# A Perceiver kernel on one core: seven more value units projected early, and a one-head cross attention whose scores lie with keys on partitions

## The chip, the cores and the metric

The kernel runs on one core of one Trainium2 chip. The metric is the device time of one execution in microseconds (us), median of three executions. Engines are called by the names of the profile: PE is TensorE (PEld its weight loads), DVE is VectorE, ACT is ScalarE, POOL is GpSimd, and SP is SyncE, whose queue issues every DMA of this kernel.

## What is computed

Twelve layers update `x` (128 tokens x 256). Each is `x = x + layer(layernorm(x), ...)`: four groups (L0 to L3) of a cross attention ("x"), a self attention ("a") and a feed-forward layer ("f"). The cross attentions read a context `ctx_1024` of 12544 rows x 256, the same for all. The change touches three of them:

```python
# L0x: a linear layer on x and on the mean of the context
# L1x: ONE head, the keys and the values are the context rows themselves
#   score[q, key] = sum_d (x[q,d]*w3[d] + w2[d]) * ctx[key,d]  +  row[q]
#   attended[q]   = softmax over the 12544 keys of score, times ctx
#   bat           = softmax over the queries of each query's largest score;  hc = bat-weighted mean of x
#   out           = [x, attended, x*attended, x*hc] @ W_qv + b
# L2x: 16 heads of 16
def _L2_xattn_ref(Q, K, V, mask, Wq, bq, Wk, bk, Wv, bv, Wo, bo):
    q = _split_heads(Q @ Wq.T + bq)
    k = _split_heads(K @ Wk.T + bk)
    v = _split_heads(V @ Wv.T + bv)          # V is the context: the "value units" below are pieces of this
    scores = jnp.einsum('bhqd,bhkd->bhqk', q, k) * scale
    scores = jnp.where(mask == 0, -jnp.inf, scores)
    attn = jax.nn.softmax(scores, axis=-1)
    return jnp.einsum('bhqk,bhkd->bhqd', attn, v)...  @ Wo.T + bo
```

All of it is in fp32.

## The kernel before, in words

The context is cut into 7 chunks of 1792 keys (`NC`, `CH`), each in two halves of 896 (`HC`). A **value unit** (c, b) is 256 keys of chunk c times `Wv` of L2x: 4 matmul instructions of 128x256 (each shows as two MATMUL records in the trace, since fp32 takes two passes), 7 units a chunk, 49 in all. A unit depends only on the context and `Wv`, so it can be made long before L2x. Every engine runs its own instruction list in the order in which the code writes it; semaphores join them.

- **L0x** (0 to 41 us) streams the 7 chunks for the mean. While a chunk is in SBUF, PE projects units b = 0 and 1 of chunks 0, 2, 3, 4, 5 and 6 (`PASSING`, L1095). **L0a** (41 to 72 us) fills PE's waits with the 5 units of `AFTER` (`after`, L730, taken by ACT at L1428). `KEPT["L2x"]` says how many units of each chunk are made ahead; they lie in `arena` and `mask_bias`, and SP writes them to DRAM (`held_out`) with two DMAs (L508, L509), which stand in SP's queue ahead of the first experts of L0f. Where there is no such work PE runs `warm` (L702), products of the identity that nobody reads.
- **L0f** (75.8 to 139 us): 8 experts of 1408 KB up and 768 KB down weights, 3 buffers in `wide`; L696 is the up product, L1034 the down product.
- **L1x** (139 to 256 us). First pass: 14 halves; for each, the query matrix `x2T` is the stationary operand and the keys are streamed (L1200: 512 and 384 columns, two halves of the depth), so a score tile is 128 queries x 896 keys. DVE (L2064) adds `row`, writes the tile to `arena` and takes its largest value. Then the largest score of each query is known along the free axis (L2068, L2069). Second pass: ACT exponentiates a tile with the accumulated sum (L1497), PE turns its 7 blocks (`turn`, L691), DVE and ACT copy them from PSUM to `pT` (L2081, L1507), and PE multiplies the turned blocks by the context rows (`multiply`, L1229). SP loads the halves (L451, L517) and the rows (L535, four buffers in `wide`). Between the passes PE has `warm(T2[:, 1], 20)`.
- **L1a, L1f** (256 to 314 us): chunk 1's seven units of L2x are made here (`early`, L714).
- **L2x** (314 to 843 us): `cross`. A prologue projects the keys and the values of chunk 0 (`key_unit` L826, `value_unit` L839), then 56 pairs of heads (7 chunks x 8 pairs) each do scores (L854), softmax, 7 groups of 4 turns (L868), and the product with the values (`multiply`, L891). The plan (`Plan.values_of`) puts the missing value units of chunk c+1 into pairs 0, 2, 3, 4 and 6 of chunk c. Kept units come back from DRAM (`load_held`, L564). **L3x** has the same form and keeps none.

Of the kernel before, what the change touches and what calls it, by code (L numbers as in the profile page):

```python
# [17 lines left out]
ALU = mybir.AluOpType  # L18
ACT = mybir.ActivationFunctionType
# [61 lines left out]
def stage_lists(layers):  # L81
# [7 lines left out]
    for layer in layers:  # L89
# [21 lines left out]
        elif layer == "L1x":  # L111
            add(layer, dve=["A", "AT", "max", "gmax", "bat", "f", "fT"], pe=["AT_ps", "hc_ps", "fT_ps", "out"],
                pool=["gmax"], act=["bat"])
# [29 lines left out]
WHOLE = 4  # L143
KEPT = {"L2x": [0 if c == 1 else 7 if c == WHOLE else 2 for c in range(7)], "L3x": [0] * 7}
# [53 lines left out]
DUMPED = 4  # L198
# [4 lines left out]
assert KD * D + (len(HELD) - IN_ARENA) * 2 * D <= CH  # L203
# [4 lines left out]
def build(nc, a, layers=LAYERS):  # L208
    ctx = ExitStack()
    with ctx:  # L210
# [179 lines left out]
        for layer in layers:  # L390
            if layer == "L0x":
                sems(layer, "first_in0", "first_in1", "first_in2", "second_in0", "second_in1", "second_in2",
                     "first_summed", "second_summed", "wv_in", "held_ready", "held_taken", "held_out",
                     "after_ready", "after_taken")
            elif layer == "L1x":
                sems(layer, "ctx_in0", "ctx_in1", "ctx_in2", "ctx_in3", "s_ready", "s_taken", "p_ready", "nat_in0", "nat_in1", "nat_in2", "nat_in3", "t_ready", "t_dve", "t_act",
# [16 lines left out]
        held_b = mask_bias[:, KD * D:KD * D + (len(HELD) - IN_ARENA) * 2 * D].rearrange("p (u n) -> p u n", n=2 * D)  # L413

        def held(of):

            n = HELD.index(of)
            return held_a[:, n] if n < IN_ARENA else held_b[:, n - IN_ARENA]
# [8 lines left out]
        def _(sp):  # L427
# [51 lines left out]

            def load_early(of):  # L480
# [8 lines left out]
            for i, layer in enumerate(layers):  # L489
                prev = layers[i - 1] if i else None  # L490
                if layer == "L0x":
# [14 lines left out]
                    sp.wait_ge(s["held_taken"], len(PASSING))  # L506
                    sp.wait_ge(s["after_taken"], len(AFTER))
                    sp.dma_start(held_out[:, 0:IN_ARENA], held_a).then_inc(s["held_out"], 16)  # L508
                    sp.dma_start(held_out[:, IN_ARENA:len(HELD)], held_b).then_inc(s["held_out"], 16)  # L509
                elif layer == "L1x":  # L510
# [13 lines left out]
                    if i + 1 < len(layers):  # L524
                        load_pack(layers[i + 1])
                    with sp.Fori(1, NC // 2) as n:
# [10 lines left out]
                    for n in range(2 * NC):  # L537
                        if n >= 4:
                            sp.wait_ge(s["pv_ready"], n - 3)
                        load_nat(n)  # L540
                    sp.wait_ge(s["s_ready"], 2 * NC)
                    load_early("L2x")
                elif layer in ("L2x", "L3x"):
# [14 lines left out]
                    def load_held(c):  # L558

                        n, units = HELD.index((c, 0)), plan.kept[c]  # L560
                        sp.wait_ge(L["L0x"]["held_out"], 32)
# [73 lines left out]
                elif layer in FF:  # L635
# [5 lines left out]
                    for e in range(n, E):  # L641
# [3 lines left out]
                        load_down(layer, e)  # L645
                if i + 1 < len(layers) and layers[i + 1] != "L3f" and (layers[i + 1] in FF or layers[i + 1] == "L1f"):

                    if prev:
                        need(sp, "dve", f"{prev}.end")
# [1549 lines left out]
```

## Time and profile before

| what | value |
|---|---|
| median of three executions | 1581.24 us (1580.27 to 1581.38) |
| the profiled execution, its own time | 1574.64 us |
| its span in the profile | 1573.0 us |
| PE / PEld busy | 1498.3 us (95%) / 1125.8 us (72%) |
| DVE / ACT busy | 957.5 us (61%) / 941.3 us (60%) |
| shares of the chain that ended last | PE 81%, DVE 7%, issue 5%, ACT 5%, DMA 2% |
| HBM read / written | 161.33 MB / 4.59 MB |

The chain that ended last is followed back from the last instruction to what released each one; a share of 81% for PE says that for that part of the span the end waited for matmuls. Times inside the text are microseconds from the start of the span.

### The profile page before, as it was taken

To read this page: it belongs to the slowest core of one execution; us is meant where nothing else is said; L and a number is where in the kernel's file an instruction comes from. 1 tells how busy PE (TensorE), PEld (TensorE's weight loads), DVE (VectorE), ACT (ScalarE), POOL (GpSimd) and SP (SyncE) were. 2 spreads that over 40 slices of the span, in tenths; PEclk is the share of its full clock that TensorE was granted. 3 is DMA by queue.
4 is the path that set the end of the run, shared out by engine and by line. 5 is a ranking of instruction groups with operands and counts; after the bars stand their busy time and mean duration, and the time that the engine had idled before them with its cause. 6 is when DMAs were issued, how large, how long until landed. Compare 5 with 4: busy or idle time off the path is not lost.

```text
span 1573.0 us, 34356 instructions
## 1 busy us (share of the span) xinstructions
PE 1498.3 (95%) x14142; PEld 1125.8 (72%) x14142; DVE 957.5 (61%) x1828; ACT 941.3 (60%) x1439; POOL 9.7 (1%) x22
## 2 busy tenths in 40 slices
PE   6999998999999999999998999999999999998899
PEld 5797587767777766777776876777777777776664
DVE  5523323658767787777775216776767676767632
ACT  3110041248887888787883215877777777778711
POOL 0000000000000000000000000000000000000000
PEclk9999999899999999999999999999999999999999
DMA  9595764274534353444314547443434343423346
GB/s 394 230 371 217 277 219 193 84 264 152 183 133 171 129 189 126 147 160 144 114 47 168 210 176 253 146 162 117 143 119 141 118 142 118 142 95 124 128 178 265
DMA packets 56169, 270.88 MB, mean 172 GB/s; under 512 B 6608, under 2 KB 6864, under 8 KB 49360
## 3 DMA queue, kind: packets, MB, share of 16 engines
q1 hardware_dynamic: 56016, 268.70, 46.5%
q8 instruction: 113, 1.85, 0.5%
q14 instruction: 40, 0.33, 0.1%
HBM read 161.33 MB, written 4.59 MB: 105 GB/s over the span
## 4 chain that ended last, share of the span: by engine, by line
PE 81%; DVE 7%; issue 5%; ACT 5%; DMA 2%; POOL 0%; SPq 0%; DVEq 0%; ACTq 0%
PE T L868 14%; PE O L891 9%; PE S L854 8%; PE O L868 7%; PE T L826 7%; PE T L839 5%; PE S L696 5%; PE O L826 3%; PE S L1200 3%; PE O L1229 3%; PE O L696 2%; PE T L691 2%; PE O L839 2%; ACT sc L1315 2%; DVE sc L1742 2%
## 5 line engine op out<-in xcount | busy, mean ns | idle before, releaser
L1742 DVE CUSTOM_DVE_ANT_0 sc<-S,mask_bias,small 128x896 f32<-128x896 f32 x336 | 377.5, 1149 | 46.9 <-PE S L854 46.9
L1315 ACT ACTIVATE sc<-sc,small 128x1792 f32<-128x1792 f32 x168 | 300.1, 1786 | 2.5 <-DVE small L1742 1.0
L1301 ACT ACTIVATE pT<-T 128x512 f32<-128x512 f32 x366 | 212.3, 597 | 87.3 <-PE T L868 87.3
L868 PE MATMUL T<-consts,sc 128*128 128x128 f32 x1546 | 232.7, 281 | 5.0 <-ACT sc L1315 3.1
L891 PEld LDWEIGHTS O<-pT,arena 128*32 128x32 f32 x6272 | 164.8, 110 | 74.8 <-issue 72.3
L868 PEld LDWEIGHTS T<-consts,sc 128*128 128x128 f32 x1546 | 168.9, 141 | 61.0 <-issue 39.8
L891 PE MATMUL O<-pT,arena 128*32 128x128 f32 x6272 | 194.4, 274 | 9.0 <-ACT pT L1301 9.0
L854 PE MATMUL S<-keys,q 64*128 64x512 f32 (+1 forms) x896 | 151.2, 414 | 10.1 <-DVE small L1742 9.9
L1708 DVE COPY pT<-T 128x512 f32<-128x512 f32 x150 | 103.5, 690 | 79.4 <-PE T L868 78.6
L1301 ACT ACTIVATE pT<-O 128x512 f32<-128x512 f32 x194 | 115.9, 597 | 52.4 <-PE O L868 52.4
L826 PE MATMUL T<-ctx_in,packs 128*128 128x448 f32 x320 | 135.1, 547 | 1.1 <-issue 1.1
L868 PE MATMUL O<-consts,sc 128*128 128x128 f32 x806 | 129.3, 281 | 1.6 <-ACT pT L1301 1.4
L1742 DVE CUSTOM_DVE_ANT_0 packs<-S,mask_bias,small 128x896 f32<-128x896 f32 x112 | 128.1, 1144 | 0.0
L868 PEld LDWEIGHTS O<-consts,sc 128*128 128x128 f32 x806 | 89.2, 141 | 33.4 <-issue 24.3
L854 PEld LDWEIGHTS S<-keys,q 64*128 64x128 f32 x896 | 67.2, 185 | 50.3 <-issue 40.4
L1315 ACT ACTIVATE packs<-packs,small 128x1792 f32<-128x1792 f32 x56 | 99.6, 1779 | 0.0
L839 PE MATMUL T<-packs,ctx_in 128*128 128x256 f32 x384 | 90.3, 379 | 0.0
L826 PEld LDWEIGHTS T<-ctx_in,packs 128*128 128x128 f32 x320 | 55.7, 192 | 35.5 <-issue 35.5
L868 PE MATMUL T<-consts,packs 128*128 128x128 f32 x518 | 78.8, 280 | 1.7 <-ACT pT L1301 1.7
L839 PEld LDWEIGHTS T<-packs,ctx_in 128*128 128x128 f32 x384 | 69.7, 190 | 7.7
L1708 DVE COPY pT<-O 128x512 f32<-128x512 f32 x74 | 51.0, 690 | 35.5 <-PE O L868 34.8
L696 PEld LDWEIGHTS S<-xT,wide 128*128 128x128 f32 x608 | 69.5, 192 | 2.3 <-issue 2.0
(369 smaller groups left out, 1803.1 us busy)
## 6 DMA issues: line engine op xcount, KB each, us to landing
keys<-keys_hl SPq DMA_DIRECT2D x224, 448.0 KB, 4.4
ctx_in<-in_ctx_cols SPq DMA_DIRECT2D x46, 896.0 KB, 4.7
wide<-in_ctx_rows SPq DMA_DIRECT2D x14, 896.0 KB, 4.6
wide<-in_up_L0f SPq DMA_DIRECT2D x8, 1408.0 KB, 13.0
sc<-in_ctx_cols SPq DMA_DIRECT2D x10, 896.0 KB, 5.5
wide<-in_up_L2f SPq DMA_DIRECT2D x8, 1024.0 KB, 7.1
wide<-in_down_L2f SPq DMA_DIRECT2D x8, 1024.0 KB, 5.0
wide<-in_up_L3f SPq DMA_DIRECT2D x4, 2048.0 KB, 8.1
```

The lines of the kernel that those rows point to most:

```text
L696: last = mm(out, lhsT[:, k, :], rhs[:, k, :], start=(k == 0), stop=(k == n - 1))
L826: last = mm(ring(plan, u)[:, 0:HC // 2], wk[:, k, hf * P:(hf + 1) * P], ctx_in[:, nb // 2, k, (nb % 2) * (HC // 2):(nb % 2 + 1) * (HC // 2 ...
L839: last = mm(ring(plan, u)[:, (t % 2) * D:(t % 2 + 1) * D], ctx_in[:, half, k, at * P:(at + 1) * P], wv[:, k, :], start=(k == 0), stop=(k = ...
L854: last = mm(S4f[:, i * 2 * BANK + n0:i * 2 * BANK + n1], q4[own, j, :], keys4[own, j, half * HC + n0:half * HC + n1], start=True, stop=True)
L868: last = nc.tensor.transpose(ring(plan, u)[:, t * P:(t + 1) * P], weights_of(2 * m + i)[:, b * P:(b + 1) * P], ident)
L891: last = mm(O2[32 * g:32 * g + 32, 1, at:at + P], vv[:, c % 2, b, j * 32:(j + 1) * 32], pT2[:, t * P:(t + 1) * P], start=(b < 4), stop=(b ...
L1200: last = mm(S4f[:, q % 2 * 2 * BANK + n0:q % 2 * 2 * BANK + n1], x2T[:, k, :], half_in(q)[:, k, n0:n1], start=(k == 0), stop=(k == KD - 1))
L1229: last = mm(O2[:, 0, 0:D], pT[:, 2 * (n % 2) + t // 4, t % 4 * P:(t % 4 + 1) * P], wide[:, (n % 4) * HC * KD + t * D:(n % 4) * HC * KD + ( ...
L1301: nc.scalar.activation(pT2[:, g * BANK:(g + 1) * BANK], ring(plan, u), ACT.Copy).then_inc(s["t_act"], 1)
L1315: nc.scalar.activation(weights_of(n), weights_of(n), ACT.Exp, bias=n_best[c % 2][:, h:h + 1], scale=-1.0, accum_out=l_new[c % 2][:, h:h + ...
L1708: V.tensor_copy(pT2[:, g * BANK:(g + 1) * BANK], ring(plan, u)).then_inc(s["t_dve"], 1)
L1742: V.tensor_tensor_reduce(weights_of(n)[:, i * HC:(i + 1) * HC], S4f[:, n % 2 * 2 * BANK:n % 2 * 2 * BANK + HC], mask_bias[:, i * HC:(i + 1 ...
```

## The change

Kept value units of L2x go from 17 to 24 (`KEPT["L2x"]` from `[2, 0, 2, 2, 7, 2, 2]` to `[4, 0, 2, 2, 7, 2, 7]`): units 2 and 3 of chunk 0, and 2 to 6 of chunk 6. Three of them, (6,2) to (6,4), join `AFTER` in L0a; four are `LATE` and are made in L1x, from halves of the context that L1x has in SBUF. The prologue of L2x then has 3 value units in place of 5, and chunk 5 none in place of 5. The dumps are one DMA of 256 KB for each unit (2 KB a partition) in place of two large ones: 17 ahead of L0f's experts, 3 at L0f's end, 4 in L1x.

L1x is rewritten: each block of 128 keys is now the stationary operand and the queries are streamed, so a score tile has keys on partitions. ACT moves it to `arena`, DVE keeps an elementwise maximum (`folded`); after the last half the fold goes over the 7 blocks, through a PE transpose and a reduction, and the broadcast maximum is turned into `T2[:, 1]`. The second pass subtracts it (`lower`, DVE), exponentiates in place (ACT), adds up the sums elementwise (`add_up`, DVE) and multiplies at once: no turns and no copies of turned blocks. The sum over keys is 7 one-column products at the end (`total_ps`). ACT now loads the table of Exp inside L1x.

```diff
-KEPT = {"L2x": [0 if c == 1 else 7 if c == WHOLE else 2 for c in range(7)], "L3x": [0] * 7}
+KEPT = {"L2x": [4, 0, 2, 2, 7, 2, 7], "L3x": [0] * 7}
+LATE = [(0, 2), (0, 3), (6, 5), (6, 6)]
...
-AFTER = [(c, b) for c, b in HELD if b >= 2]
+AFTER = [(c, b) for c, b in HELD if b >= 2 and (c, b) not in LATE]
+FIRST_OUT = PASSING + AFTER[0:5]
...
+            def dump(units, done):
+                for u in units:
+                    sp.dma_start(held_out[:, HELD.index(u)], held(u)).then_inc(L["L0x"][done], 16)
...
                     load_pack(layers[1])
-                    sp.wait_ge(s["held_taken"], len(PASSING))
-                    sp.wait_ge(s["after_taken"], len(AFTER))
-                    sp.dma_start(held_out[:, 0:IN_ARENA], held_a).then_inc(s["held_out"], 16)
-                    sp.dma_start(held_out[:, IN_ARENA:len(HELD)], held_b).then_inc(s["held_out"], 16)
...
+                    if layers[i + 1] == "L0f":
+                        sp.wait_ge(L["L0x"]["held_taken"], len(PASSING))
+                        sp.wait_ge(L["L0x"]["after_taken"], 5)
+                        dump(FIRST_OUT, "held_out")
...
+                elif layer == "L1x":
+                    late(0, S4[:, 2])
+                    warm(T2[:, 0], 7)
                 elif layer != layers[0]:
                     warm(T2[:, 0], 11)
...
                     after(1, S4[:, 3])
-                    warm(T2[:, 1], 5)
+                    after(2, S4[:, 1])
...
+                elif layer == "L0a":
+                    after(7, S4[:, 1])
                 else:
                     warm(S4[:, 0], wait)
...
-                        pe.wait_ge(L["L0x"]["after_taken"], len(AFTER))
-                        warm(O2[:, 1], 11)
+                        after(6, T2[:, 1], 4)
+                        warm(O2[:, 0], 8)
+                        pe.wait_ge(L["L0x"]["after_taken"], 6)
...
-                        for n0, n1 in ((0, BANK), (BANK, HC)):
-                            for k in range(KD):
-                                last = mm(S4f[:, q % 2 * 2 * BANK + n0:q % 2 * 2 * BANK + n1], x2T[:, k, :],
-                                          half_in(q)[:, k, n0:n1], start=(k == 0), stop=(k == KD - 1))
+                        for t in range(TH):
+                            last = product(S4f[:, n % 2 * 2 * BANK + t * P:n % 2 * 2 * BANK + (t + 1) * P],
+                                           half_in(q)[:, :, t * P:(t + 1) * P], x2T)
...
-                    warm(T2[:, 1], 20)
-                    turn(0)
-                    for n in range(1, 2 * NC):
-                        turn(n)
-                        multiply(n - 1)
+                    late(2, O2[:, 0])
+                    need(pe, "dve", f"{layer}.fold")
+                    done("pe", transposes(T2[:, 0], work[:, 0:P], 1), f"{layer}.fold_ps")
+                    need(pe, "dve", f"{layer}.m")
+                    done("pe", transposes(T2[:, 1], work[:, 256:256 + P], 1), f"{layer}.m_ps")
...
+                    late(3, O2[:, 1])
+                    pe.wait_ge(L["L0x"]["late_taken"], 3)
+                    for n in range(2 * NC):
+                        multiply(n)
...
+                    need(pe, "dve", f"{layer}.total")
+                    for t in range(TH):
+                        last = mm(S4[:, 2, 0:1], sc[:, 2, t * P:(t + 1) * P], work[:, 512 + D:512 + D + 1],
+                                  start=(t == 0), stop=(t == TH - 1))
+                    done("pe", last, f"{layer}.total_ps")
...
...
+                    def lower(n):
+                        at = n * HC
+                        dve.wait_ge(s["moved"], n + 1)
+                        for n0, n1 in ((0, 4 * P), (4 * P, HC)) if n == 0 else ((0, HC),):
+                            piece = arena[:, at + n0:at + n1].rearrange("p (t n) -> p t n", n=P)
+                            V.tensor_tensor(piece, piece, bcast(T2[:, 1, 0:P], (n1 - n0) // P, False), ALU.subtract) \
+                                .then_inc(s["lowered"], 1)
+                    def add_up(n):
+                        dve.wait_ge(s["p_ready"], n + 2)
+                        other = arena[:, 0:HC] if n == 1 else folded
+                        ins = V.tensor_tensor(folded, other, arena[:, n * HC:(n + 1) * HC], ALU.add)
```

How the change moves instructions, as the two programs have them. **PE, from the end of L0f to the second pass of L1x.** `T`, `O` and `S` are PSUM; line numbers are those of each file. Before (the same four rows of L1200 go on through a loop), from the last product of L0f's experts:

```order
L1034 MATMUL O<-wide,arena 128x256 x12
L702 MATMUL T<-consts 128x128 x11
L691 MATMUL T<-consts,xn 128x128 x2
L702 MATMUL O<-consts 128x128 x9
L691 MATMUL T<-consts,x 128x128 x2
L1200 MATMUL S<-ctx_in,x2T 128x512 x2
L1200 MATMUL S<-ctx_in,x2T 128x384 x2
...
L702 MATMUL T<-consts 128x128 x20
L691 MATMUL T<-consts,sc 128x128 x14
L1229 MATMUL O<-wide,pT 128x256 x7
L691 MATMUL T<-consts,sc 128x128 x7
```

And in the changed kernel (L774 is `late`, L730 `warm`, L719 transposes, L1276 `multiply`):

```order
L1085 MATMUL O<-wide,arena 128x256 x12
L774 MATMUL S<-mask_bias,ctx_in 128x256 x4
L730 MATMUL T<-consts 128x128 x7
L719 MATMUL T<-consts,xn 128x128 x2
L774 MATMUL S<-mask_bias,ctx_in 128x256 x4
L719 MATMUL T<-consts,x 128x128 x2
L724 MATMUL S<-x2T,ctx_in 128x128 x28
...
L774 MATMUL O<-mask_bias,ctx_in 128x256 x4
L719 MATMUL T<-consts,work 128x128 x2
L774 MATMUL O<-mask_bias,ctx_in 128x256 x4
L1276 MATMUL O<-wide,arena 128x256 x21
```

The 7 turns before every group of 7 products are gone, a half of the first pass is 14 products of 128 columns in place of 4 of 512 or 384, and the 20 products of `warm` between the passes are replaced by two late units and two single transposes.

**SP, between L0a's weights and L0f's experts**, with the semaphores that each waits for. Before:

```order
L435 DMA packs<-in_pack_L0a 128x4352
L508 DMA held_values<-arena 128x7680 [waits L0x_after_taken,L0x_held_taken]
L509 DMA held_values<-mask_bias 128x1024
L435 DMA packs<-in_pack_L0f 128x16 [waits dve_stages]
L456 DMA wide<-in_up_L0f 128x2816 [waits dve_stages]
```

And now:

```order
L448 DMA packs<-in_pack_L0a 128x4352
L448 DMA packs<-in_pack_L0f 128x16 [waits dve_stages]
L496 DMA held_values<-arena 128x512 [waits L0x_after_taken,L0x_held_taken]
L496 DMA held_values<-arena 128x512 x9
L496 DMA held_values<-mask_bias 128x512 x2
L496 DMA held_values<-arena 128x512 x5
L469 DMA wide<-in_up_L0f 128x2816 [waits dve_stages]
```

Two DMAs ahead of the first expert's weights have become seventeen, with the same bytes.

**ACT, in L1x.** Now (L1552 takes a late unit, L1562 moves a score tile, L1572 is Exp):

```order
L1552 ACTIVATE mask_bias<-S 128x512 x2
L1562 ACTIVATE arena<-S 128x896 x14
L1552 ACTIVATE wide<-O 128x512
L1572 ACT_TABLE_LOAD
L1572 ACTIVATE arena<-arena 128x512
L1572 ACTIVATE arena<-arena 128x384
L1552 ACTIVATE wide<-O 128x512
L1572 ACTIVATE arena<-arena 128x896
```

Before, the table load stood right behind the last expert's activations of L0f; now it stands between the 14 moves and the first Exp.

## Rows read from the trace of the kernel before

**Rows 1.** The page, its busy line and the chain that ended last.

```profile
PE 1498.3 (95%) x14142; PEld 1125.8 (72%) x14142; DVE 957.5 (61%) x1828; ACT 941.3 (60%) x1439; POOL 9.7 (1%) x22
...
PE 81%; DVE 7%; issue 5%; ACT 5%; DMA 2%; POOL 0%; SPq 0%; DVEq 0%; ACTq 0%
```

**Rows 2.** The chain in order of time: start us, us, engine, output, line, records.

```profile
64.71 3.49 PE O L1127 x32
...
96.60 5.11 PE S L696 x44
...
145.91 42.36 PE S L1200 x112
196.09 3.02 PE O L1229 x14
199.88 3.02 PE O L1229 x14
```

**Rows 3.** Timeline, L1x: start, us, engine, line, operation, records [idle before <-releaser].

```profile
142.11 0.44 PE L691 MATMUL T<-consts,xn 128*128 128x128 f32 x2 [0.40 <-DVE xn L1535]
...
188.11 4.63 PE L702 MATMUL T<-consts 128*128 128x128 f32 x40
...
195.92 3.19 PE L1229 MATMUL O<-wide,pT 128*128 128x256 f32 x14
...
248.14 0.48 DVE L2098 TENSOR_SCALAR arena<-O,small 128x256 f32<-128x256 f32 x1 [5.48 <-PE O L1229]
```

**Rows 4.** Stretches: us, busy (x records) of PE, PEld, DVE, ACT, POOL, PEclk, DMA share, GB/s.

```profile
322.00:324.00 2.00, 2.00 (x8) 1.19 (x7) 0.75 (x2) 0.92 (x2) 0.00 (x0) 1.00 0.36 140
...
559.86:626.81 66.95, 65.77 (x785) 47.28 (x785) 54.51 (x103) 57.20 (x86) 0.00 (x0) 1.00 0.51 180
...
702.08:777.35 75.27, 74.09 (x826) 54.76 (x825) 54.96 (x103) 60.62 (x91) 0.00 (x0) 1.00 0.38 130
...
292.00:296.00 4.00, 2.90 (x9) 2.12 (x9) 3.04 (x4) 0.00 (x0) 0.00 (x0) 0.50 0.00 0
```

**Rows 5.** Timeline, the prologue of L2x.

```profile
327.12 1.89 PE L839 MATMUL T<-packs,ctx_in 128*128 128x256 f32 x8
...
335.85 0.67 PE L854 MATMUL S<-keys,q 64*128 64x512 f32 x4
```

**Rows 6.** Timeline, L0a and the start of L0f.

```profile
58.26 2.72 PE L702 MATMUL O<-consts 128*128 128x128 f32 x22
...
61.01 3.70 PE L806 MATMUL S<-pT,arena 128*128 128x512 f32 x8
...
75.79 10.13 PE L696 MATMUL S<-xT,wide 128*128 128x128 f32 x88
```

**Rows 7.** DMA issues: size of one, us from issue to landing (the experts' from 60:60.5).

```profile
held_values<-arena SPq DMA_DIRECT2D x1, 3840.0 KB, 12.2
...
mask_bias<-in_pack_L3x SPq DMA_DIRECT2D x1, 256.0 KB, 2.5
...
wide<-in_up_L0f SPq DMA_DIRECT2D x1, 1408.0 KB, 15.3
```

**Rows 8.** DMA queue in 176:190 and 324.5:333: packets, MB, share of 16 engines.

```profile
q1 hardware_dynamic: 796, 5.03, 89.1%
...
q1 hardware_dynamic: 951, 3.01, 102.7%
```

**Rows 9.** Timeline, prices of DVE and ACT forms in L0a and L1a.

```profile
54.67 0.69 DVE L1902 TENSOR_TENSOR work<-work,x 128x512 f32<-128x512 f32 x1
...
57.61 0.60 ACT L1428 ACTIVATE arena<-S 128x512 f32<-128x512 f32 x1 [1.13 <-PE S L730]
58.61 2.35 DVE L1585 TENSOR_TENSOR pT<-T,consts 128x1024 f32<-128x1024 f32 x2
...
268.45 1.28 ACT L1450 ACT_TABLE_LOAD   x1
...
269.75 0.23 ACT L1450 ACTIVATE small<-small 128x32 f32<-128x32 f32 x1
```

More of the change, by code:

```diff
@@ L732, in after, with late @@
                 last.then_inc(s["after_ready"], 1)
+            def late(n, bank):
+                s = L["L0x"]
+                c, b = LATE[n]
+                halves = L["L1x"]
+                if c == 0:
+                    pe.wait_ge(halves["ctx_in0"], 16)
+                    if 2 * b + 1 >= TB // 2:
+                        pe.wait_ge(halves["ctx_in1"], 16)
+                for t in (2 * b, 2 * b + 1):
+                    part, at = divmod(t, TB // 2)
+                    for k in range(KD):
+                        last = mm(bank[:, (t % 2) * D:(t % 2 + 1) * D], ctx_in[:, part, k, at * P:(at + 1) * P],
+                                  early_wv[:, k, :], start=(k == 0), stop=(k == KD - 1))
+                last.then_inc(s["late_ready"], 1)
             def norm(layer):
@@ L1123, in _ @@
                         pe.wait_ge(L["L3x"]["early_taken"], 4)
+                    else:
+                        pe.wait_ge(L["L0x"]["after_taken"], 7)
                     for b in range(4):
@@ L1186, in _ @@
                     s = L[layer]
-                    warm(O2[:, 1], 9)
+                    late(1, S4[:, 3])
                     need(pe, "dve", f"{layer}.A")
@@ L1411, in take_early, with take_after @@
                                      ACT.Copy).then_inc(s["early_taken"], 1)
+            def take_after(n, bank):
+                act.wait_ge(L["L0x"]["after_ready"], n + 1)
+                nc.scalar.activation(held(AFTER[n]), bank, ACT.Copy).then_inc(L["L0x"]["after_taken"], 1)
             for layer in layers:
@@ L2067, in _ @@
-                    dve.wait_ge(s["s_taken"], 2 * NC)
-                    link(V.tensor_reduce(row_max, maxes, X, ALU.max))
-                    done("dve", V.tensor_scalar(rec, row_max, -1.0, None, ALU.mult), f"{layer}.max")
+                    folded = sc[:, 2, 0:HC]
+                    fold, fold_last = work[:, 0:P], work[:, P:2 * P]
+                    for n in range(2 * NC):
+                        last = n == 2 * NC - 1
+                        dve.wait_ge(s["s_ready" if last else "moved"], n + 1)
+                        src = S4f[:, n % 2 * 2 * BANK:n % 2 * 2 * BANK + HC] if last else arena[:, n * HC:(n + 1) * HC]
+                        if n:
+                            dve.wait_ge(s["s_taken"], n)
+                        if n == 0:
+                            V.tensor_copy(folded, src).then_inc(s["s_taken"], 1)
+                        elif not last:
+                            V.tensor_tensor(folded, src, folded, ALU.max).then_inc(s["s_taken"], 1)
+                            if n == 2 * NC - 2:
+                                dve.wait_ge(s["s_taken"], n + 1)
+                                link(V.tensor_reduce(fold, folded.rearrange("p (t n) -> p n t", n=P), X, ALU.max))
+                        else:
+                            V.tensor_reduce(fold_last, src.rearrange("p (t n) -> p n t", n=P), X, ALU.max) \
+                                .then_inc(s["s_taken"], 1)
@@ L2090, in _ @@
+                    for n in range(1, 2 * NC):
+                        if n + 2 < 2 * NC:
+                            lower(n + 2)
+                        add_up(n)
+                        if n == 4:
                             need(dve, "pe", f"{layer}.hc_ps")
```

186 lines of the change are left out of this document (107 added, 79 removed).

## The prediction

> **What bounds the kernel now.** I read the page first: PE is busy for 95% of the span and carries 81% of the chain that ended last [rows 1], so a change pays where it takes matmuls off PE, or a wait of PE's. Then the chain in order of time, for L1x: the first pass is one run of PE, 112 records of L1200 in 42.2 us from 145.91 to 188.11, 3.01 us a half, and the second repeats with a period of 3.79 us, of which the products with the context are 3.02 and the turns and their handover the rest [rows 2, 3]. Then the stretches of L2x: chunk 5 with five value units takes 75.27 us, chunk 3, which has none, 66.95, both with PE busy for over 98% [rows 4]. Last the timelines around L0f's start, between the passes of L1x, and in L2x's prologue.
>
> This is summed against the profiled execution, 1574.64 us. The three runs have the median 1581.24, 6.6 us above it; I take the difference over unchanged.
>
> **L0a and the norm of L1x: +1.1.** A value unit on PE is 1.75 us (five in 8.73 us from 327.12 to 335.85 [rows 5]); a record of `warm` is 0.12 (22 in 2.72 [rows 6]).
> - Second norm of L0a: a unit in place of 10 warm records, 0.5 longer, mostly inside DVE's normalisation. I take 0.1.
> - Ahead of the head products: a unit (from 58.1) and 16 warm records (1.9) in place of 22. PE is free at 61.75, where it began L806 at 61.01 [rows 6]: +0.7. L0a's tail: the unit ends as DVE's result comes, 0.
> - First norm of L1x: 1.75 + 14 x 0.12 from 139.0 is 142.4, the transposes began at 142.11 [rows 3]: +0.3. `late(1)` (1.75) is shorter than the 18 records that it replaces, 0.
>
> **The dumps ahead of L0f: 0.** They now go in 17 DMAs with rows of 2 KB. The first expert's weights landed 15.3 us after their issue at 60.1, that is at 75.4, and PE began with them at 75.79 [rows 6, 7]: only 0.4 of slack, so this counts. Against it, the dumps wait for five units of `AFTER`, and one unit was moved earlier, so they start 1.7 sooner; and L0a ends 0.8 later. Price of the small rows: a packet took 250 ns in the stretch whose packets average 6.3 KB (796 packets, 89.1% of 16 engines x 14 us) and 147 ns where they average 3.2 KB (951, 102.7% of 16 x 8.5 us) [rows 8], 33 ns for each KB, so one of 2 KB is an estimated 110 ns; 17 x 128 of them on 16 engines make 15.0 us. Before, the dumps took about 13.2 (from 58.8 to the landing of the weights less 3.4 for their own bytes). 1.8 us more against 0.4 + 1.7 + 0.8 of slack: hidden. Bounds: 0, and +4 if small packets cost twice what I put on them over the large ones.
>
> **First pass of L1x: +3.3.** Weights of 128x128 with 128 moving columns are exactly L0f's up product: 44 records in 5.11 us, 0.116 each [rows 2]. A half is 14 calls, 28 records, 3.25 us, against 3.01: 14 x 3.25 = 45.5 against 42.2. ACT's move of 896 columns (about 0.9, from 0.60 for 512 [rows 9]) and DVE's maximum (about 1.1, from 0.69 for 512 [rows 9]) hide beside it. The late dumps are 0.5 MB beside PE's pass; cover enough.
>
> **Between the passes: -3.0.** Before, 188.11 to 195.92, 7.8 us [rows 3]. Now, from the last half's end: DVE's reduction of it to +1.2 and the last maximum to +1.45, `late(2)` on PE to +1.95, a transpose to +2.2, reduction and broadcast copy to +2.75, transpose to +3.2, `lower` of 512 columns to +3.9 (0.69 [rows 9]), Exp to +4.6, product at about +4.8. The table load (1.28 [rows 9]) runs from +2.7, behind `late(2)`'s copy, and is done at +4.0, just in time. A load from 268.45 is followed by the next activation at 269.75, 0.02 us behind its end [rows 9]. The Trainium skill, page "ScalarE: Activation LUTs", section "What ACT_TABLE_LOAD costs", adds a drain of 1380 ns to each switch; by that Exp would start at +5.4 and the sum would be 1.4 us smaller. The row does not bear it out, so the sum goes by 1.28.
>
> **Second pass: -9.3.** 14 groups at 3.02 plus 0.5 for the batch product: 42.8, against 52.1 (195.92 to 248.03). This holds if DVE keeps up: `lower` with PSUM as one operand about 1.05 (1024 columns take 1.17 [rows 9]), `add_up` 1.1, 2.2 us a half against 3.02. Exp, on ACT, costs about what the move does. The context rows arrive at 0.9 MB every 3.02 us, 304 GB/s, under the 403 GB/s which the stretch 176:190 reaches at full share (5.03 MB in 14 x 0.89 us [rows 8]).
>
> **Tail of L1x: +1.8.** DVE began the division at 248.14, 0.1 behind the last product. Now 14 one-column records stand between, at the 0.11 of L1127's 17-column records (32 in 3.49 [rows 2]), 1.6, and a reciprocal of 0.2.
>
> **Prologue of L2x: -3.5.** Two units of 1.75. The scores then want the first half's keys at 332.3. The queue was at 0.36 share in 322:324 [rows 4], so the 0.5 MB more of kept values (1.2 us) fits into that gap and the key copies start when they did. Bounds: -3.5 and 0.
>
> **Chunk 5: -8.3.** 75.27 - 66.95 [rows 4]. The load of seven units for chunk 6 is what chunk 4 does now. Certain but for a few tenths.
>
> Sum: 1.1 + 0 + 3.3 - 3.0 - 9.3 + 1.8 - 3.5 - 8.3 = **-17.9 us**. Profiled execution 1556.7, median **1563.3 us**, -1.1%. A change under 0.2%, about 3 us, could not be told from none.
>
> **Rivals.**
> - *L0f starts late.* The dumps run slower than estimated and every microsecond beyond 1.1 spare goes on the path. For: the spare is small, and the second expert has no more. Against: the earlier start. At +4: 1567.3. Chance 0.15.
> - *DVE bounds the second pass.* If the broadcast operand of `lower` makes both operations cost 1.7 us, the period is 3.5, +0.5 x 12 = +6: 1569.3. No row shows more than 1.2 for such a form. 0.06.
> - *L2x's prologue waits for its keys,* so the two units come out of a wait: +3.5, 1566.8. For: DMA share is about 1.0 from 324 to 333. Against: before, nothing waited there, PE came from its value units straight to the scores [rows 5]. 0.10.
> - *PE's clock falls elsewhere.* It was granted 0.50 (1.2 GHz) in 292:296, where PE was busy 2.90 of 4 us [rows 4]; the same work two stages later may meet it for more or less of the time, and L1x's tail now has matmuls of one column. 2 us either way, in the range; no case of its own.
> - *The small dumps do not overlap (slower).* If each 256 KB dump is finished before the next moves, it costs at least the 2.5 us of such a DMA [rows 7]: 17 x 2.5 = 42.5 us in place of 13.2, less 2.9 of slack, L0f starts 26.4 us late: and the median is 1589.7. It decides against the change from 34 us for the dumps, 2.0 each. Against: the key copies, 448 KB each, have four in flight and reach a share of 1.0 [rows 8]. The Trainium skill, page "DMA: Bandwidth & Descriptors", section "Bandwidth", says to batch DMAs to 1 MiB or more for 75% of peak, which speaks against this edit; its fit in "Anatomy of one DMA" makes 256 KB an estimated 2.6 us, 44 us for 17 in a row, with 17 x 2.6 - 16.1 the sum would end at +10 and the median at 1591. No row here shows DMAs of one queue kept apart. 0.03.
> - *The gain is there but the shift sets off other waits* (1567 to 1573), 0.06.
>
> **How the numbers follow.** Forecast 0.60; the cases above 0.15, 0.06, 0.10, 0.03, 0.06. The likeliest gives 1563.3. Eight in ten: downward the clock and a faster handover between the passes, 4 us; upward the late L0f and the prologue together, 7.5 us: 1559.3 to 1570.8. Faster by more than 0.2%: 0.95; within: 0.02; slower: 0.03.
>
> **What would show it.** In the profile after: first pass 45 to 46 us, PE solid; the first product 4.5 to 5.5 us behind its end; groups of 14 products 3.02 apart with no idle PE; division 1.8 us behind the last; L0f's first product within 1 us of where L0a's end puts it, else the dumps are the cause; five units' worth, 8.3 us, missing in chunk 5; the first scores of L2x right behind three value units. Wrong if the second pass's period is over 3.2 us, if ACT waits behind its table load, or if PE idles ahead of L0f's first product.

## The result, and the profile after

| what | before | after |
|---|---|---|
| median | 1580.76 us (4 executions: 1575.37, 1580.27, 1581.24, 1581.38) | 1556.03 us (4: 1554.82, 1555.73, 1556.34, 1559.02) |
| the profiled execution, its span | 1574.64, 1573.0 us | 1554.82, 1553.0 us |
| mean granted clock of the profiled execution | 0.992 | 0.992 |

The ratio is 0.9854, with a 95% interval of 0.9828 to 0.988: 1.5% faster. I had said 1563.3 us (1559.3 to 1570.8), so the sign was right and the gain was larger than even the low end. Against the profiled execution, on which the sum was made, I had said 1556.7 and 1554.82 came.

The page of the changed kernel, its busy line and chain (against [rows 1]):

```profile
PE 1480.4 (95%) x14248; PEld 1129.8 (73%) x14248; DVE 976.6 (63%) x1830; ACT 945.6 (61%) x1426; POOL 9.7 (1%) x22
...
PE 80%; DVE 8%; issue 5%; ACT 5%; DMA 2%; POOL 0%; SPq 0%; DVEq 0%; ACTq 0%
```

PE is still the bound, with 17.9 us less busy time, and DVE has 19.1 us more. The chain of L1x in order of time (start us, us, what), against [rows 2, 3]:

```profile
146.00 40.93 PE S L724 x364
186.92 0.02 issue
186.95 0.93 ACT arena L1562
187.87 0.02 issue
187.90 1.10 DVE sc L2140
189.00 0.02 issue
189.02 1.71 DVE work L2143
190.74 0.02 issue
190.76 1.10 DVE work L2145
...
193.37 1.28 ACT L1572
194.65 0.01 issue
194.66 0.64 ACT arena L1572
```

The chain leaves PE a half early, at 186.9: from there DVE decides when the second pass can begin, and last the table load. The timeline of the turnaround, the second pass and the tail (start, us, engine, line, operation, records [idle before <-releaser]):

```profile
189.87 1.89 PE L774 MATMUL O<-mask_bias,ctx_in 128*128 128x256 f32 x8
190.76 1.09 DVE L2145 TENSOR_REDUCE work<-S 128x128 f32<-128x896 f32 x1
195.44 9.30 PE L1276 MATMUL O<-wide,arena 128*128 128x256 f32 x42 [0.17 <-ACT arena L1572]
...
205.01 33.40 PE L1276 MATMUL O<-wide,arena 128*128 128x256 f32 x154
...
238.25 1.62 PE L1292 MATMUL S<-work,sc 128*128 128x1 f32 x14
239.90 0.17 DVE L2195 RECIPROCAL small<-S 128x1 f32<-128x1 f32 x1 [15.77 <-PE S L1292]
240.11 0.48 DVE L2197 TENSOR_SCALAR sc<-O,small 128x256 f32<-128x256 f32 x1
```

The late unit of L774 stands directly behind the last scores, so the first pass ends at 189.87. DVE has the last scores there too, but begins to reduce them at 190.76. The second pass is two runs of L1276, 196 records (14 halves of 14), with only the two records of the batch product between them, and 14 records take 3.02 us as forecast. In the tail the reciprocal's 15.77 us of idle time say that DVE's own part of the sum was ready long before.

The prologue of L2x (against [rows 5]) and chunk 5 of L2x (691.94 to 758.90, with chunk 3 above it; against [rows 4]):

```profile
320.38 1.89 PE L890 MATMUL T<-packs,ctx_in 128*128 128x256 f32 x8
322.11 1.89 PE L890 MATMUL O<-packs,ctx_in 128*128 128x256 f32 x8
323.84 1.89 PE L890 MATMUL T<-packs,ctx_in 128*128 128x256 f32 x8
325.66 0.67 PE L905 MATMUL S<-keys,q 64*128 64x512 f32 x4
```

```profile
549.72:616.67 66.95, 65.77 (x786) 47.31 (x785) 54.53 (x103) 57.21 (x86) 0.00 (x0) 1.00 0.50 180
691.94:758.90 66.96, 65.77 (x786) 47.30 (x785) 54.53 (x103) 57.22 (x86) 0.00 (x0) 1.00 0.47 166
```

Three units and then the scores, without a gap; and chunk 5 is now chunk 3 to 0.01 us.

**Where the time went**, by the same place in both traces:

| step | before | after | said | measured |
|---|---|---|---|---|
| start of the first pass | 145.91 | 146.00 | +1.1 | +0.1 (the stream of L0x ended 0.6 sooner this time; +0.7 without that) |
| first pass | 42.2 | 43.87 | +3.3 | +1.7 |
| between the passes | 7.81 | 5.57 | -3.0 | -2.2 |
| second pass | 52.1 | 42.8 | -9.3 | -9.3 |
| last product to division | 0.1 | 1.86 | +1.8 | +1.8 |
| L1a and L1f (half clock there longer) | | | none | +1.3 |
| prologue of L2x | | | -3.5 | -3.5 |
| chunk 5 of L2x | 75.27 | 66.96 | -8.3 | -8.3 |
| behind chunk 5 (before had a half clock at 844) | | | none | -1.5 |
| sum | 1573.0 | 1553.0 | -17.9 | -20.0 |

The last row but one is this stretch of before (us, busy (x records) of PE, PEld, DVE, ACT, POOL, PEclk, DMA share, GB/s), which has no like in the profile after:

```profile
844.00:846.00 2.00, 2.00 (x6) 1.58 (x5) 1.19 (x4) 0.00 (x0) 0.39 (x1) 0.51 0.06 10
846.00:848.00 2.00, 2.00 (x10) 1.71 (x9) 0.41 (x1) 0.46 (x1) 0.16 (x1) 0.64 0.87 267
```

The clock is at its lower level (1.2 GHz of 2.4) for most of this, which takes 2 x 0.49 + 2 x 0.36 = 1.7 us from PE. So step by step the mechanism is the one forecast, and the sum is off by 2.1 us in all; single terms are off by up to 1.6, and the half clock added 1.3 in L1a and L1f and saved 1.5 behind chunk 5. What is left is that the medians lie 24.7 us apart and the two profiled executions 19.8, and the experiments began there.

### The profile page after: what moved, and what is told of

It is laid out like the page before. It is cut to its first block, busy times and chain, and to the rows that moved or that the text cites. A ratio compares the mean times of both kernels' runs of the same rounds, so it can differ in the third digit from the quotient of the medians.

```text
span 1553.0 us, 34523 instructions
## 1 busy us (share of the span) xinstructions
PE 1480.4 (95%) x14248; PEld 1129.8 (73%) x14248; DVE 976.6 (63%) x1830; ACT 945.6 (61%) x1426; POOL 9.7 (1%) x22
## 4 chain that ended last, share of the span: by engine, by line
PE 80%; DVE 8%; issue 5%; ACT 5%; DMA 2%; POOL 0%; SPq 0%; DVEq 0%; ACTq 0%
PE T L919 14%; PE O L942 9%; PE S L724 8%; PE S L905 8%; PE O L919 7%; PE T L877 7%; PE T L890 5%; PE O L1276 3%; PE O L877 3%; PE O L724 2%; PE O L890 2%; ACT sc L1366 2%; PE S L1014 2%; DVE sc L1811 2%; PE T L719 2%
## 5 line engine op out<-in xcount | busy, mean ns | idle before, releaser
L1352 ACT ACTIVATE pT<-T 128x512 f32<-128x512 f32 x360 | 208.9, 598 | 82.6 <-PE T L919 82.6
L1777 DVE COPY pT<-T 128x512 f32<-128x512 f32 x155 | 106.9, 690 | 85.8 <-PE T L919 85.2
L905 PE MATMUL S<-keys,q 64*128 64x512 f32 (+1 forms) x896 | 150.9, 414 | 10.2 <-DVE small L1811 10.0
L1352 ACT ACTIVATE pT<-O 128x512 f32<-128x512 f32 x200 | 119.5, 597 | 55.2 <-PE O L919 55.2
L877 PE MATMUL T<-ctx_in,packs 128*128 128x448 f32 x332 | 140.2, 547 | 1.1 <-issue 1.1
L890 PE MATMUL T<-packs,ctx_in 128*128 128x256 f32 x328 | 77.2, 379 | 0.0
L724 PE MATMUL S<-xT,wide 128*128 128x128 f32 x608 | 70.9, 276 | 0.0
L919 PEld LDWEIGHTS T<-consts,packs 128*128 128x128 f32 x516 | 56.4, 141 | 15.1 <-issue 9.8
```

Source lines behind the costliest of these rows:

```text
L724: last = mm(out, lhsT[:, k, :], rhs[:, k, :], start=(k == 0), stop=(k == n - 1))
L877: last = mm(ring(plan, u)[:, 0:HC // 2], wk[:, k, hf * P:(hf + 1) * P], ctx_in[:, nb // 2, k, (nb % 2) * (HC // 2):(nb % 2 + 1) * (HC // 2 ...
L890: last = mm(ring(plan, u)[:, (t % 2) * D:(t % 2 + 1) * D], ctx_in[:, half, k, at * P:(at + 1) * P], wv[:, k, :], start=(k == 0), stop=(k = ...
L905: last = mm(S4f[:, i * 2 * BANK + n0:i * 2 * BANK + n1], q4[own, j, :], keys4[own, j, half * HC + n0:half * HC + n1], start=True, stop=True)
L919: last = nc.tensor.transpose(ring(plan, u)[:, t * P:(t + 1) * P], weights_of(2 * m + i)[:, b * P:(b + 1) * P], ident)
L1352: nc.scalar.activation(pT2[:, g * BANK:(g + 1) * BANK], ring(plan, u), ACT.Copy).then_inc(s["t_act"], 1)
```

## Experiments

**How times are compared here.** Executions of one kernel scatter widely (those of before from 1574.3 to 1588.5 us). Each comes with its span and mean granted clock, and their product is the time that it would have taken at the full clock, called the full-clock time below. It is an estimate (the clock has three digits, and not every microsecond is PE's), but its mean is steadier than a median. The +- behind it is the standard error of that mean.

**1. Both kernels again, unchanged.**

> The kernel before, unchanged, to see its own scatter. Theory A: its executions lie on two levels, 1574.5 to 1576 and 1580 to 1582 us, as the five times known so far do (1574.64, 1575.37, 1580.27, 1581.24, 1581.38), and the upper level has a lower mean granted clock (about 0.988 against 0.992), so the 6.6 us between its profiled execution and its median is TensorE time at the half clock, and no property that a change keeps. Theory B: the timed executions all lie at 1580 to 1582 and only the profiled one is shorter; then the offset belongs to the way of timing, and the changed kernel's own 1.2 us would need another reason.

> The changed kernel, unchanged. Theory A: 1554.5 to 1559.5 us, median near 1556, with the longer ones at a lower mean clock (0.989 against 0.992). Theory B: all timed executions within 1 us of each other.

Measured: the kernel before 1574.3 to 1583.15 us, median 1578.4 of 12. The executions at 0.992 took 1574.3 to 1575.3 and those at 0.986 and 0.987 took 1581.3 to 1583.2, with all values between: not two levels, but a time that goes with the clock. The changed kernel took 1556.95 and 1557.15 (0.992), 1560.46 (0.989) and 1561.35 (0.988). Theory A stands in what matters and B falls; but two of these four lie above the 1559.5 that I had given as their upper end, and their median, 1558.8, above the 1556. With the runs of before that came beside all later experiments there are 74 executions of it (median 1578.8, full-clock 1560.1 +-0.1) and 8 of the changed kernel (median 1557.1, full-clock 1541.6 +-0.4): the change is worth **18.6 us at equal clock**, where the sum said 17.9. At 0.992 alone the means are 1575.1 (10) and 1556.2 (5), 18.9 apart.

**2. L1x alone, and the seven units made but not used.** The first is the kernel before with the new L1x, without `late`. The second is the changed kernel with one line:

```diff
-        self.kept = KEPT[layer]
+        self.kept = [2, 0, 2, 2, 7, 2, 2] if layer == "L2x" else KEPT[layer]
```

> The kernel before with the rewritten L1x only: 17 kept value units, the two large dumps and the prologue and chunk 5 of L2x as before; warm products stand where the late units stood. By the two traces L1x is worth 8.1 us (its last products -8.03 against before, of which L0a and the start +0.1): profiled execution 1566.5 us, L2x 1.3 us earlier or later by the clock. My forecast's terms (first pass +3.3, between -3.0, second -9.3, tail +1.8) would make it 1567.4. If the units made in L1x cost it time, for example through DMA or ACT, this comes out lower, under 1565.

> The changed kernel, which makes and dumps all 24 units, but L2x's plan takes only the old 17 from DRAM and projects the other seven again in its prologue and in chunk 5. By the trace these seven are worth 3.5 + 8.3 = 11.8 us: profiled execution 1566.6 us, within 1 us of the run with L1x alone, since making the units early costs only the 0.6 us by which the head products of L0a start later. Rival: the units take part of their gain back where they are made (L0a, L1x, the dumps); then this run is longer than the one with L1x alone by over 1.5 us.

Measured: medians 1570.2 us and 1571.5 us, both 0.9949 of before (0.9935 to 0.9964), full-clock 1551.9 +-0.4 and 1553.0 +-0.3. L1x alone gains 8.2 (said 8.1). Using the seven units gains 11.4 (1553.0 to 1541.6; said 11.8), making them costs 1.1 +-0.5 (said 0.6; the rival's 1.5 is not excluded by this). The parts add up by construction, since each run is compared with the one before it; what is tested is the size of each. Both profiled executions had the clock at 0.989, which is why their own times, 1569.8 and 1571.5, are 3 and 5 us above what I wrote.

**3. The tail of L1x.**

```diff
+ # DVE, behind the last add_up
+ V.tensor_reduce(fold, folded.rearrange("p (t n) -> p n t", n=P), X, ALU.add)
  # PE, ahead of the last multiply; the seven products behind it are gone
+ mm(S4[:, 2, 0:1], work[:, 0:P], work[:, 512 + D:512 + D + 1], start=True, stop=True)
```

> The changed kernel with the sum over keys folded on DVE first (one reduction over the 7 blocks, DVE being idle for 15.8 us there), so that one one-column product, put ahead of the last half's products, takes the place of seven behind them. If the tail's +1.8 us is the 14 records and the reciprocal behind the last product, the division begins 0.1 us behind that product in place of 1.86, and L1x's tail (last product to the output product) is 1.5 us shorter with the one product's 0.2 counted. Rival: the tail is bound by DVE's own chain, and nothing changes.

Measured: the timeline of DVE in this kernel,

```profile
240.55 0.17 DVE L2195 RECIPROCAL small<-S 128x1 f32<-128x1 f32 x1 [9.68 <-PE S L1286]
243.75 0.48 DVE L2197 TENSOR_SCALAR sc<-O,small 128x256 f32<-128x256 f32 x1 [3.03 <-PE O L1276]
```

The reciprocal is done 3 us early and the division waits for the last product. From the first product of the second pass to the output product it is 47.6 us (200.45 to 248.06) in place of 49.0 (195.44 to 244.42): -1.4, where 1.5 was said. Median 1556.7, full-clock 1539.8 +-0.3, -1.8 +-0.5. The term was the 14 records.

**4. The turnaround of L1x.** The fold over blocks one half earlier, the last two halves reduced straight from PSUM; and an Exp of one column behind the 12th move.

```diff
-                            if n == 2 * NC - 2:
+                            if n == 2 * NC - 3:
                                 link(V.tensor_reduce(fold, folded..., X, ALU.max))
+                        elif not last:
+                            V.tensor_reduce(fold_last, src..., X, ALU.max)
+                            link(V.tensor_tensor(fold, fold, fold_last, ALU.max))
...
+                        if n == 2 * NC - 3:
+                            nc.scalar.activation(bat, row, ACT.Exp, scale=0.0)
```

> The changed kernel with the fold of the maximum over its 7 blocks made one half earlier, in DVE's idle time, and the last two halves reduced straight from PSUM. If DVE's 1.70 us reduction is what makes the turnaround 5.6 us in place of the 4.8 forecast, the last half's reduction starts as its scores end and the first product comes 0.8 us sooner (4.8 behind the end of the first pass). Rival: ACT's table load holds the first Exp, as it ended 0.01 us before it; the load stands behind the last half's move, which waits for DVE too, so it should move along; if it doesn't, the gain is under 0.3.

> As the run before, and an Exp of one column behind the 12th move makes ACT load the table there, ahead of the turnaround. If the load then holds Exp, this gives 0.3 to 0.4 us more, 4.5 us from the end of the first pass to the first product, where late unit 3 on PE (1.75 us from the second transpose) becomes the last thing. If the load is hidden anyway, no difference.

Measured, from the end of the first pass to the first product: 5.57 us in the changed kernel, 4.93 (191.90 to 196.83) with the early fold, 4.60 (189.90 to 194.50) with the table too. The timeline of the last, ACT's load and DVE's last reductions:

```profile
183.85 0.92 ACT L1562 ACTIVATE arena<-S 128x896 f32<-128x896 f32 x1 [2.21 <-PE S L724]
184.78 1.28 ACT L1565 ACT_TABLE_LOAD   x1
186.08 0.20 ACT L1565 ACTIVATE small<-small 128x1 f32<-128x1 f32 x1
```

```profile
187.98 1.09 DVE L2148 TENSOR_REDUCE work<-S 128x128 f32<-128x896 f32 x1 [0.34 <-ACT arena L1562]
...
190.16 1.09 DVE L2153 TENSOR_REDUCE work<-S 128x128 f32<-128x896 f32 x1 [0.76 <-PE S L724]
```

DVE now waits for PE (0.76 us), not the other way round, and the last reduction starts 0.26 behind the end of the scores in place of 0.89. So the late fold was worth 0.64 and the load 0.33, as said within 0.2. The medians, 1557.5 and 1558.7, do not show it; the full-clock times, 1539.7 +-0.3 and 1540.0 +-0.5, are 1.9 +-0.5 and 1.6 +-0.6 below the changed kernel's. The second fits the 1.0 of the trace; the first is more than its 0.6 by over two standard errors, so the sizes are read from the traces. Both profiles had a half clock at 240 to 248, in the tail with the one-column products (3 of 10 profiles with these products had it, 0 of 4 of the new L1x without; the numbers are too small to call it an effect).

**5. The three edits together.**

> All three edits on the changed kernel: 1.5 + 1.1 = 2.6 us less than the changed kernel at the same mean clock, 1552.2 us for a profiled execution at 0.992. The median should be 1554.5 by the eight executions of the changed kernel known so far (median 1557.1).

Measured: median **1553.24 us** (1551.58 to 1555.75), ratio to before 0.9835 (0.9815 to 0.9855), span 1551.4 at a clock of 0.993, full-clock 1539.3 +-0.5. From the first pass to the output product L1x takes 96.1 us (148.10 to 244.16) in place of 98.4: -2.4 of the 2.6 said. The median came 1.3 below the 1554.5 said, but the profiled execution 1.0 above the 1552.2, at a clock that was no lower: its span times clock, 1540.5, is no better than that of the first profile of the changed kernel, 1540.6. So the gain rests on the stretch of L1x and on the means of five and eight executions, 2.2 +-0.6 at equal clock. It has the lowest median of the case.

**6. A half clock in front of L0f.** Comparing profiles showed what the profiled execution had not: in most of the changed kernel's the clock falls at the end of L0a. The windows 66:68 to 70:72 of the changed kernel run again, and behind them its timeline of PE there, with the unit as it was in the first profile as the last line:

```profile
66.00:68.00 2.00, 2.00 (x20) 2.00 (x20) 0.00 (x0) 0.00 (x0) 0.00 (x0) 1.00 0.66 246
68.00:70.00 2.00, 2.00 (x10) 1.82 (x10) 1.02 (x4) 0.00 (x0) 0.00 (x0) 0.62 1.01 345
70.00:72.00 2.00, 2.00 (x6) 1.55 (x6) 0.28 (x1) 0.00 (x0) 0.00 (x0) 0.53 1.05 371
```

```profile
65.09 3.75 PE L1181 MATMUL O<-arena,sc 128*128 128x17 f32 x32
68.68 3.55 PE L758 MATMUL S<-mask_bias,ctx_in 128*128 128x256 f32 x8
72.07 0.38 PE L719 MATMUL T<-consts,x 128*128 128x128 f32 x2
...
67.86 1.97 PE L758 MATMUL S<-mask_bias,ctx_in 128*128 128x256 f32 x8
```

The unit in the tail takes 3.55 us in place of 1.97, is no longer done when DVE's result comes, and L0f's first product moves to 78.11, from 75.71. I first held the start of L0a's head products to decide it (late ones had the fall, early ones not). The edits: in the changed kernel and in the one with the three edits `warm(O2[:, 0], 8)` became 5; in the kernel before `warm(O2[:, 1], 11)` became 15.

> The changed kernel with 10 warm records in place of 16 ahead of L0a's head products. In ten profiles so far the clock fell to its half somewhere in 66 to 80 and L0f began 2 to 5 us late whenever these products started at 61.36 or later (5 of 7 profiles with the changed L0a), and never where they started at 61.01 or earlier. Theory P: it is when the products start that decides; they now start at 60.3 to 61.1, nothing falls in 66 to 80, L0f's first product comes at 75.1 to 75.9, and the median is some 1.5 us below the changed kernel's 1557.1. Theory Q: it is the value unit in L0a's tail; then the clock falls as often and the median stays.

> All three edits of L1x and the 10 warm records. Theory P: no half clock in 66 to 80, and 1 us or so below the run with the three edits alone (1553.2): 1552. Theory Q: the same as that run.

> The kernel before with 30 warm records in place of 22 ahead of L0a's head products, which then start at 61.6 to 62.0. Theory P: the clock falls in 66 to 80 here too, L0f begins 2.5 us late or more (78.2), and the median is 2 to 4 us above before's. Theory Q: no fall, since there is no unit in the tail; L0f's first product at 76.6, median 0.9 us above before's.

Measured: theory P falls. With the trim the head products began at 61.20 and 60.68 (the second earlier than in four of the five earlier profiles without a fall), and the clock fell in both; the kernel before began them at 61.30, and it did not fall. L0f's first product came at 75.97 there, where theory Q said 76.6. Medians 1556.0, 1554.7 and 1578.3 us, full-clock 1541.3, 1539.3 and 1560.9: nothing gained by the trim. The delay cost 0.7 +-0.3 by the full-clock time; the ratio, 1.0002 (0.9982 to 1.0022), doesn't show it.

Then the unit itself. It was made ahead of the head products, in place of the 8 calls of `warm`, with `warm` back in the tail and there a wait of PE for ACT's copy of the unit (the same with the three edits); and the kernel before got four products of 256 columns in its tail, whose results nobody reads.

> The changed kernel with the unit of L0a's tail, (6,4), made ahead of the head products, in place of the 16 warm records there; the tail has the 10 warm records of before. If that unit in the tail is what lets the clock fall in 66 to 80 (8 of 11 profiles of kernels with it, 0 of 4 without), no half clock appears there and L0f's first product comes at 75.2 to 76.2. Rival R: it is the whole of the changed L0a (two more units, no wait of PE from 61 on), and the clock falls as before; L0f's first product at 77.5 or later.

> The run with the moved unit once more, for a second profile: the same expectation, no half clock in 66 to 80 if the tail's unit is the cause, half clock in most profiles if it is not.

> The three edits of L1x and the moved unit. If the tail's unit was the cause: median 1552 us, and no execution with 1.7 us or more of half clock in 66 to 80. By rival R the same as the three edits alone, 1553.2.

> The kernel before with 4 products of 256 columns, the work of a value unit, in L0a's tail in place of the 10 warm records; its results are not used. If the unit in the tail is the cause, the half clock appears in 66 to 80 in this one too and L0f begins 2 us late or more in most executions; median 1 to 2 us above before's. By rival R nothing falls there and the median is before's.

All profiles together (the cost is the sum of what the granted clock lacks to 1.00 in 66 to 80):

| L0a | L0f's first product, no fall | with a fall (its cost) |
|---|---|---|
| as before | 75.79, 75.50, 75.24 | |
| as before, 8 records more | 75.97 | |
| as before, products of 256 in the tail | | 78.03 (3.4) |
| changed | 75.71, 75.75 | 78.11, 77.74, 77.83, 77.75, 77.51 (1.7 each); 79.31 (3.4); 80.73, 79.89 (5.1) |
| changed, unit ahead of the head products | | 77.08 (1.7); 80.64, 79.94 (5.1) |

The fall came in 11 of 13 profiles with the changed L0a (8 of 10 when the last expectations were written, which count 11) and in 0 of 4 with `warm` alone. Moving the unit did not stop it, and in the one profile of the kernel before with its like in the tail the fall was there. So it goes with more products of 256 columns in L0a, wherever they stand; the tail's unit is not the sole cause. The eight more records of `warm` did not bring it, in one profile. Why more work gets less clock there is open. The time of the whole kernel does not show the fall: where the products were put into the kernel before, 1 to 2 us more were expected and its 12 executions took 0.9999 of before (0.9987 to 1.0012), at a mean clock of 0.9901 against 0.9895 for the 17 of before beside them; and with the unit moved and the three edits 1552 was expected. Medians: 1559.3 and 1553.5 (unit moved), 1577.5 (before with the products); full-clock 1540.8 +-0.3, 1538.8 +-0.3 and 1561.0 +-0.3.

**7. Four dumps more ahead of L0f.** `held_out` got four more places, and four units were written a second time.

> The changed kernel with four of the units dumped a second time, to a spare place in DRAM, so that 21 DMAs of 256 KB stand ahead of L0f's experts. My price for one was 0.88 us (15.0 for 17). The weights landed at 74.2 and were used at 75.7, 1.5 us of slack: the first product of L0f should come 4 x 0.88 - 1.5 = 2.0 us late, at 77.7, and an execution without a half clock ahead of it should be about 2 us longer at that point. Rival: the experts' weights overlap the dumps, and it comes less than 1 us late.

Measured: 1557.04 us. The first weights landed at 77.17 (issued at 70.27, 6.9 us), against 74.2 in the changed kernel, whose L0a ran 0.25 sooner: 0.68 us for each dump, not 0.88. L0f began at 77.51; this profile had a fall of 1.7, and the others with such a one began at 77.08 to 78.11. So the four dumps cost nothing here: PE waited for DVE until 77.08, and the weights were there 0.3 us before their use. That 77.51 is near the 77.7 expected is luck, since the clock brought it and not the dumps. What they cost without a fall this run doesn't show; by its landing at 77.17 against a start at 75.96 (75.71 and the 0.25) I estimate 1.2 us, not 2.0.

## Why the prediction was right or wrong

- **The step that failed** is "I take the difference over unchanged". The 6.6 us between the profiled execution and the median of before were read as a property of the measurement. They were the difference between an execution at 0.992 and three at a lower clock (by the 74 executions, 1580 to 1581 us is 0.987 to 0.989). The changed kernel's four had 0.992, 0.992, 0.992 and 0.989, and its median lay 1.2 above its profile. That is 5.4 of the 7.3 us of the miss. By the larger samples (medians 1578.8 and 1557.1) the step from profile to median is 4.2 us before and 2.2 after: of the 5.4 us, 2.4 are the draw of before's three executions, 1.0 is the draw of the changed kernel's four, and 2.0 are a clock that the two kernels do not share. The other 1.9 us of the miss are the sum's own (1556.7 against 1554.82), from the terms below. The range took in 2 us for the clock, "either way", although three given times and a profiled one stood 6 us apart: they called for at least that much.
- **Part of the clock is the kernel's.** The 52 executions of kernels with all seven units used have a mean clock of 0.9905, the 98 of the kernel before and its two variants 0.9892: some 2 us that no term had. The two kernels of experiment 2, with 0.9888 and 0.9895, lie with the kernel before. The profiles don't show where: within their spans the half clock costs 10.2 to 23.0 us in the one group and 12.0 to 15.8 in the other. This stays open.
- **First pass, +3.3 said, +1.7 measured.** I took 44 records in 5.11 us as 0.116 each. But the length of a run of records holds the end of its last one. The chain has 364 records in 40.93 us, 0.112, and 14 x 28 of these make the 43.9 measured, under the "45 to 46" of the forecast. A run of 44 overstated the price by the 0.2 us at its end (16 records from 59.15 last 1.95 us, but the next group starts after 1.78).
- **Between the passes, -3.0 said, -2.2 measured.** The turnaround was listed from the last half's end, and DVE was taken to be free then. It still had the maximum of the half before and its fold, 1.70 us by L2143, and came 0.9 late. Experiment 4 gave 0.64 of it back. The 5.57 us lie just outside the "4.5 to 5.5" of the forecast.
- **Table load.** Said: done just in time. Measured: it ends at 194.65 and Exp starts at 194.66, so ACT did wait behind it, which the prediction had as a sign of being wrong; with the load elsewhere 0.33 us come back. The row agrees with [rows 9] and again not with the drain of 1380 ns that the Trainium skill, page "ScalarE: Activation LUTs", section "What ACT_TABLE_LOAD costs", adds to each switch: here 0.01 us stands between load and Exp.
- **Second pass, tail, prologue, chunk 5** came as said to 0.1 us. Experiment 2 confirms L1x and the units by taking the units out or leaving them unused, experiment 3 the tail by replacing it; the first pass and the second were not changed by themselves, and are read from the traces alone.
- **L0a and the norms, +1.1 said, +0.7 measured**; but "L0a's tail: the unit ends as DVE's result comes, 0" holds only at the full clock. In 11 of 13 profiles the rival "L0f starts late" is what happened, by 1.4 us and more against 75.7, through the clock and not through the dumps; whether it made the kernel longer, experiment 6 doesn't show.
- **The dumps, 0 said, 0 measured.** The first dump was issued at 55.90, and the weights, issued at 67.60, landed 6.6 us later, at 74.2: 18.3 us in all, where the sum had 15.0 for the dumps and 3.4 for the weights. They were there 1.5 ahead of their use. One dump more costs 0.68 (experiment 7), less than the average of 0.88. In 61 to 63 the DMA engines ran at full share with DMAs of 256 KB only (the SP queue's rows for the first dumps and for the weights, the DMA queue in 61:63):

```profile
55.90 5.83 SPq L496 DMA_DIRECT2D held_values<-arena  x10
...
67.60 0.45 SPq L469 DMA_DIRECT2D wide<-in_up_L0f  x1
...
q1 hardware_dynamic: 421, 0.77, 103.3%
```

  So the rival that small dumps do not overlap is refuted. The advice to batch to 1 MiB (the Trainium skill, page "DMA: Bandwidth & Descriptors", section "Bandwidth"), which that page gives beside loads issued from GpSimd, would have spoken against this edit; it did not decide here: the small DMAs, issued from SP, overlapped at 385 GB/s (0.77 MB in 2 us), and 1.5 us of slack were left.
- **The other rivals.** DVE does not bound the second pass (1.09 for `lower` and 1.08 for `add_up` in a half of 3.02; the rival's two operations at 1.7 would make 3.4, where 3.5 was written), and the prologue waits for no keys.

## What to carry to other kernels

Before you carry a difference between two kinds of times over, ask what varies: where TensorE is busy for 95% of the span, multiply each span by its mean clock, and compare that. Price a long run of equal instructions by a long run, or take the end of the last one off a short one. At a turnaround between two passes ask of each engine what it still has to finish from the half before, and move reductions and table loads into the idle time ahead of it; work on the path that another engine could do for nothing (14 one-column products against one reduction in DVE's 15.8 idle us) goes there.

## What the runs showed of the hardware

- The cost of the falls of the clock comes in equal portions: in 18 profiles every one, but those that the end of the span cuts, costs 1.7 us, 3.4, 5.1 or 6.8, and a profile has 6 to 13 portions of 1.7. Seven portions are 12.0 us and a mean clock of 0.992 (the two first profiles), 13 are 23 us and 0.986 (`early_fold`); the executions without a profile fit this by their clocks, as the 74 of before go from 1575.1 us at 0.992 to 1583.3 at 0.986.
- It is not idleness alone that brings them: at 68 to 72 PE was busy for 4.00 of 4 us, and the 2 us ahead of the fall, 66 to 68, for 2.00 of 2. But busy is not the same as much work: those 2 us were the 17-column products of L1181, which stand there in the kernel before too.
- A reduction on DVE over 7 blocks of 128 (128x128 out of 128x896) takes 1.70 us from SBUF and 1.09 from PSUM, as the two rows of L2143 and L2145 in the chain above show (1.71 and 1.10 with the step to the next). I had priced the one at the last half at 1.2 and overlooked the other.
